# Chunk 2 turned by DMA, rest products in pairs, and the second residual made by ScalarE and GpSimd

## The reference

```python
xn = layernorm(x)
# branch 1, per sequence
w = exp(tanh(((xn @ W + b) @ xn.T) / (|s - t| + eps)));  w[s, s] = 0
attn = (w / (w.sum(-1) + eps)) @ xn
# branch 2, per token: two of eight experts, and a shared one
scores = sigmoid(xn @ gate_w.T);  sel = top_k(scores + expert_bias, 2)
h_e = relu((score_e * xn) @ w_up[e].T) ** 2          # hidden size 176, bf16
ffn = sum over sel of h_e @ w_down[e].T + relu(xn @ shared_up.T) ** 2 @ shared_down.T
out = x + attn + ffn
```

## Time and profile before

| | us |
|---|---|
| median of 3 runs | 116.38 (115.9 to 116.49) |
| profiled execution | 116.35 |
| its span, first to last instruction | 114.5 |
| TensorE busy | 108.1 |
| VectorE busy | 100.7 |
| ScalarE busy | 88.4 |
| GpSimd busy | 71.0 |

### The profile page before, as it was taken

The page is one execution under the profiler, slowest core; times in us unless marked ns, Lnnn a source line. Parts: engine busy times, 40 slices in busy tenths (PEclk is TensorE's granted clock), DMA queues, the critical chain, the costliest instruction groups (busy, mean ns, idle before and its releaser), DMA issues.

```text
span 114.5 us, 2792 instructions
## 1 busy us (share of the span) xinstructions
PE 108.1 (94%) x898; PEld 82.6 (72%) x898; DVE 100.7 (88%) x319; ACT 88.4 (77%) x136; POOL 71.0 (62%) x134
## 2 busy tenths in 40 slices
PE   3987999969999999999999999999999999999990
PEld 3955558757787695878588777869588767859790
DVE  6979989998798989999899989998999689989751
ACT  3454899986748996888788797879788887899550
POOL 6538953599939489677969498776967610516000
PEclk9999999999999999999999999999999999999999
DMA  3999306656772769999698939893988659887983
GB/s 108 311 258 300 115 0 121 130 109 124 139 137 51 185 119 190 169 217 120 113 213 191 143 75 208 168 217 58 173 174 217 126 105 127 174 198 132 109 234 95
DMA packets 52191, 17.62 MB, mean 154 GB/s; under 512 B 49233, under 2 KB 50129, under 8 KB 52177
## 3 DMA queue, kind: packets, MB, share of 16 engines
q1 hardware_dynamic: 51600, 16.49, 72.6%
q0 software_dynamic: 288, 0.72, 3.4%
q10 hardware_dynamic: 288, 0.23, 0.6%
HBM read 3.84 MB, written 2.10 MB: 52 GB/s over the span
## 4 chain that ended last, share of the span: by engine, by line
PE 87%; DMA 5%; ACT 2%; DVE 2%; issue 1%; POOL 1%; DVEq 0%; POOLq 0%
PE out_ps L1089 16%; PE h_ps L1040 13%; PE dots L996 11%; PE side L1017 10%; PE out_ps L1077 6%; DMA hiddenT<-hidden 5%; PE out_ps L1071 5%; PE small L981 5%; PE side L1030 4%; PE out_ps L1119 4%; PE small L952 4%; PE h_ps L1053 2%; ACT hidden L563 1%; PE small L933 1%; PE side L972 1%; PE small L961 1%
## 5 line engine op out<-in xcount | busy, mean ns | idle before, releaser
L754 DVE SCALAR_TENSOR_TENSOR gated<-h_ps,gates 128x1408 bf16<-128x1408 f32 x28 | 45.2, 1615 | 3.3 <-PE h_ps L1040 2.3
L563 ACT ACTIVATE hidden<-gated 128x1408 bf16<-128x1408 bf16 x29 | 39.7, 1378 | 3.0 <-DVE gated L754 2.9
L1089 PE MATMUL out_ps<-downT,hiddenT 128*128 128x128 bf16 x341 | 22.8, 219 | 0.9 <-DMA hiddenT<-hidden 0.9
L1089 PEld LDWEIGHTS out_ps<-downT,hiddenT 128*128 128x128 bf16 x341 | 20.8, 98 | 3.3 <-DMA hiddenT<-hidden 1.1
L1040 PE MATMUL h_ps<-upT,xnTb 128*128 128x512 bf16 (+1 forms) x84 | 21.3, 362 | 0.0
L1017 PEld LDWEIGHTS side<-xn,probs 128*128 128x128 f32 x120 | 15.1, 191 | 1.5 <-issue 0.5
L1017 PE MATMUL side<-xn,probs 128*128 128x129 f32 x120 | 16.1, 276 | 0.0
L996 PE MATMUL dots<-projT,xnT 128*128 128x256 f32 x60 | 15.4, 380 | 0.0
L996 PEld LDWEIGHTS dots<-projT,xnT 128*128 128x128 f32 x60 | 11.0, 190 | 4.4 <-issue 1.7
L1040 PEld LDWEIGHTS h_ps<-upT,xnTb 128*128 128x128 bf16 x84 | 7.1, 98 | 9.6 <-issue 3.2
L357 POOL TENSOR_SCALAR_AFFINE_SELECT probs<-probs 128x256 f32<-128x256 f32 x16 | 6.6, 411 | 10.9 <-ACT probs L512 10.8
(11 more groups left out here) (122 smaller groups left out, 184.3 us busy)
## 6 DMA issues: line engine op xcount, KB each, us to landing
x_sb<-in_x SPq DMA_DIRECT2D x7, 256.0 KB, 8.1
out_y<-final SPq DMA_DIRECT2D x7, 256.0 KB, 2.3
hiddenT<-hidden SPq DMA_TRANSPOSE x31, 3.6
upT<-in_up POOLq DMA_DIRECT2D x1, 352.0 KB, 6.9
downT<-in_down POOLq DMA_DIRECT2D x1, 352.0 KB, 7.9
late_sb<-in_late SPq DMA_DIRECT2D x1, 192.0 KB, 5.2
x_sb<-in_x SPq DMA_DIRECT2D x1, 128.0 KB, 2.4
x_sb<-in_x ACTq DMA_DIRECT2D x1, 128.0 KB, 2.6
```

The source lines that it names most:

```text
L563: a.activation(hidden[:, t, :], gated[:, t, :], ACT.Square).then_inc(squared, 1)
L754: v.scalar_tensor_tensor(out=gated[:, t, :].rearrange("p (e h) -> p e h", e=E), in0=h_ps[:, 0:NH].rearrange("p (e h) -> p e h", e=E), scal ...
L1089: last = t_.matmul(out_at(c, t), hiddenT[:, c % 2, t, j, :], downT[:, j, :], start=(t == 0 and j == 0 and c < LAST), stop=((t >= 2 or c == ...
```

## The change

Four parts.

1. Chunk 2 joins the chunks that are turned by DMA: `BY_DMA` becomes a list, `transpose_x(2)` and `take_xT(2)` go, `split(2)`, `turn_planes(2)` and `merge(2)` come.
2. In the first chunks `down_tile(0, 0)` and `(0, 1)` move down in TensorE's order, behind `up_tile(1, 0)` and behind `shared_down_rest(0)`.
3. The rest products of chunks 2 and 3, 4 and 5, 6 and 7 are run in pairs: those of the odd chunk one pass earlier, into the upper half of the output banks. The odd chunk's main product takes the place of its rest products and does the waiting for the finished chunk before.
4. For chunks 1 to 6 the second sequence's residual is made like chunk 0's: ScalarE scales (`scale_second`, behind `square(c, 1)`), GpSimd adds x (`add_second_x`, behind `make_gates`), and VectorE's `attend(c)` goes. `shared_main(c)` then waits for `second_scaled`. Chunk 7 keeps VectorE's way, and `attend(7, 1)` moves behind the last up product.

```diff
-        BY_DMA = 4
+        BY_DMA = (2, 4, 5, 6, 7)
...
+        def pair_second(c):
+            return c >= 3 and c % 2 == 1
+
+        def pair_first(c):
+            return pair_second(c + 1)
+
-        def out_bank(h):
-            return out_ps[:, h * CH:h * CH + 2 * P]
+        def out_bank(c, h):
+            at = h * CH + (2 * P if pair_second(c) else 0)
+            return out_ps[:, at:at + 2 * P]
...
 # SP
+            turn_planes(2)
             for k in range(1, NCH):
                 turn(k - 1, 0)
...
 # GpSimd
-            def add_second_x():
-                pool.wait_ge(second_scaled, 1)
-                g.tensor_tensor(resid[:, 0, 2:4, :], scaled[:, 1, :, :], x_sb[:, 0, 2:4, :], ALU.add
+            def add_second_x(c):
+                pool.wait_ge(second_scaled, c + 1)
+                wait(pool, final_ready, 2 * (c - 1))
+                g.tensor_tensor(resid[:, c % 2, 2:4, :], scaled_second[:, c % 2, :, :], x_sb[:, c, 2:4, :], ALU.add
                                 ).then_inc(second_resid, 1)
...
             normalize(2, 3, 4)
+            split(2)
             mask(0, 0)
             mask(0, 1)
             square_rest(0)
+            merge(2)
             square_shared(0)
...
             add_x(1)
+            add_second_x(1)
             square_shared(1)
...
                 if f < NCH:
                     make_gates(f)
+                if c < LAST:
+                    add_second_x(c)
                 square_shared(c)
                 if f < NCH:
                     mask(f, 0)
...
 # ScalarE
-                if c == 1:
-                    act.wait_ge(second_resid, 1)
                 wait(act, first_resid, c - 1)
...
-            def scale_second():
-                act.wait_ge(attn_step, 4)
+            def scale_second(c):
+                act.wait_ge(attn_step, 2 * (Q * c + 1) + 2)
+                wait(act, second_resid, c - 1)
                 for t in range(2):
-                    last = a.activation(scaled[:, 1, t, :], attend_bank(0, 1)[:, t * (D + 1):t * (D + 1) + D],
+                    last = a.activation(scaled_second[:, c % 2, t, :],
+                                        attend_bank(c, 1)[:, t * (D + 1):t * (D + 1) + D],
                                         ACT.Identity, scale=rownorm[:, 1, t:t + 1])
                 last.then_inc(second_scaled, 1)
...
-            take_xT(2)
             take_pair(1)
...
             square(1, 1)
+            scale_second(1)
             take_pair(2)
...
                 square(c, 0)
                 square(c, 1)
+                scale_second(c)
                 take_proj(f)
...
 # VectorE
             route_mark(2)
-            attend(1)
             finish(0, 0)
...
                 attend_norm(c, 1)
-                attend(c)
                 finish(o, 0)
...
 # TensorE
                 elif c > 0:
-                    pe.wait_ge(attn_taken, c)
+                    pe.wait_ge(second_scaled, c + 1)
                 t_.matmul(shared_bank(c), supT, xnT[:, c % 4, :], start=True, stop=True).then_inc(sup_made, 1)
...
                 else:
-                    pe.wait_ge(final_ready, 2 * c)
+                    pe.wait_ge(final_ready, 2 * (c - 1) if pair_second(c) else 2 * c)
...
             def shared_down_main(c):
                 pe.wait_ge(sup_squared, c + 1)
+                if pair_second(c):
+                    pe.wait_ge(final_ready, 2 * c)
...
             dots(1, 1)
-            transpose_x(2)
             up_tile(0, 3)
             attend(0, 1)
-            down_tile(0, 0)
             rest(2)
             up_tile(1, 0)
+            down_tile(0, 0)
             attend(1, 0)
+            shared_down_rest(0)
             down_tile(0, 1)
-            shared_down_rest(0)
             transpose_exp(2)
...
                 up_tile(c, 0)
                 attend(c, 0)
-                shared_down_rest(o)
+                if pair_second(o):
+                    shared_down_main(o)
+                else:
+                    shared_down_rest(o)
+                if pair_first(o):
+                    shared_down_rest(o + 1)
                 rest(f)
                 up_tile(c, 1)
-                shared_down_main(o)
+                if not pair_second(o):
+                    shared_down_main(o)
                 down_tile(o, 2)
...
             up_by_bank(1)
             shared_down_rest(o)
+            shared_down_rest(c)
             shared_down_main(o)
             up_by_bank(2)
-            attend(c, 1)
             down_tile(o, 2)
             down_tile(o, 3)
             up_by_bank(3)
-            shared_down_rest(c)
+            attend(c, 1)
             shared_down_main(c)
```

More of the change, by code:

```diff
@@ L233, in turn_planes @@
                 sp.wait_ge(planes_split, merges(c))
-                wait(sp, xT_merged, merges(c - 2))
+                wait(sp, xT_merged, merges(c) - 2)
                 sp.dma_start_transpose(
-                    planesT[:, c % 2, :, :].rearrange("p h (t n) -> p (h t) n", n=P),
-                    planes[:, c % 2, :, :, :].rearrange("p h t d -> p (h t d)")
-                ).then_inc(planes_turned[c % 2], 16)
+                    planesT[:, plane_slot(c), :, :].rearrange("p h (t n) -> p (h t) n", n=P),
+                    planes[:, plane_slot(c), :, :, :].rearrange("p h t d -> p (h t d)")
+                ).then_inc(planes_turned[plane_slot(c)], 16)
             def store_last(h):
@@ L330, in split @@
                 pool.wait_ge(xn_ready, xns(c, TILES - 1))
-                wait(pool, planes_turned[c % 2], planes_count(c) - 16)
-                g.tensor_copy(planes[:, c % 2, :, :, :],
+                wait(pool, planes_turned[plane_slot(c)], planes_count(c) - 16)
+                g.tensor_copy(planes[:, plane_slot(c), :, :, :],
                               xn[:, c, :, 0:D].bitcast(U16).rearrange("p t (d h) -> p h t d", h=2)
@@ L341, in merge @@
                 g.tensor_copy(xnT[:, c % 4, :].bitcast(U16).rearrange("p (n h) -> p h n", h=2),
-                              planesT[:, c % 2, :, :]).then_inc(xT_merged, 1)
+                              planesT[:, plane_slot(c), :, :]).then_inc(xT_merged, 1)
             def narrow(c):
-                if c < BY_DMA:
-                    pool.wait_ge(xT_taken, c + 1)
+                if c not in BY_DMA:
+                    pool.wait_ge(xT_taken, taken(c))
                 else:
@@ L410, in _ @@
             square_first_chunk_end()
-            add_second_x()
+            add_second_x(0)
             mask(1, 1)
@@ L460, in take_xT @@
             def take_xT(c):
[L461 removed]
+                act.wait_ge(xT_made, taken(c))
                 wait(act, sup_made, c - 3)
@@ L589, in _ @@
             square(0, 2)
-            scale_second()
+            scale_second(0)
             relu_rest(2)
@@ L945, in rest @@
                     pe.wait_ge(first_half_taken, 1)
-                if c >= BY_DMA:
+                if c == 2:
+                    pe.wait_ge(expT_taken, 2)
+                elif c in BY_DMA:
                     pe.wait_ge(proj_taken, c)
+                if c in BY_DMA:
                     pe.wait_ge(xT_merged, merges(c))
                 for h in range(2):
-                    if 0 < c < BY_DMA or c == 0 and h == 1:
-                        pe.wait_ge(xT_taken, c + 1)
+                    if c in (1, 3) or c == 0 and h == 1:
+                        pe.wait_ge(xT_taken, taken(c))
                     last = t_.matmul(small[64 * h:64 * h + 64, 0:S], restT, xnT[:, c % 4, h * S:(h + 1) * S],
@@ L1070, in shared_down_rest @@
                         rows = slice(64 * h, 64 * h + 64)
+                        own_bank = c == LAST and 2 * h + i == TILES - 1
+                        bank_first = h == 1 and i == 0 and not pair_second(c)
                         t_.matmul(out_at(c, 2 * h + i), rest_hidden[rows, c % 4, i * P:(i + 1) * P],
-                                  sdown_tail[rows, :], start=((i == 0 and (h == 1 or c == LAST)) or (c == LAST and h == 1)), stop=False, skip_group_check=True)
+                                  sdown_tail[rows, :], start=(own_bank or bank_first), stop=False,
+                                  skip_group_check=True)
             def shared_down_main(c):
                 pe.wait_ge(sup_squared, c + 1)
+                if pair_second(c):
+                    pe.wait_ge(final_ready, 2 * c)
                 for t in range(TILES):
@@ L1089, in down_tile @@
                     last = t_.matmul(out_at(c, t), hiddenT[:, c % 2, t, j, :], downT[:, j, :],
-                                     start=(t == 0 and j == 0 and c < LAST),
+                                     start=(t == 0 and j == 0 and not pair_second(c)),
                                      stop=((t >= 2 or c == LAST) and j == KT - 1), skip_group_check=True)
```

25 lines of the change are left out of this document (13 added, 12 removed).

## The result

The changed kernel took 119.07 us, the median of four runs (118.75 to 119.2), against 116.37 for the kernel before beside it (115.9 to 116.49): a ratio of 1.0279, 95% interval 1.0227 to 1.0332. (The quotient of the two medians is 1.023, at the lower end of that interval; why the two differ is not on record.) That is slower by 2.7 us, where the forecast said 3.4 and 119.7. The profiled execution took 118.75 with a span of 117.0, so in the traces 2.5 us of span are to be found.

The account below looks back on a forecast made before the run. TensorE was taken to bound the kernel, with mask and `side` nearly late. Terms -0.65 + 2.65 + 1.56 - 0.2 = +3.36 us on the 114.5 span, plus 1.85, gave 119.7 us, 2.9% slower; range 116.9 to 121.0.

Parts of the forecast that it names:

- both links: `attend(f, 0)` waiting for GpSimd's mask and `shared_main(c)` for ScalarE's second scaling; both bind, chance 0.60, 118.2 to 121.0 us.
- ramp up to `attend(2, 0)`: First chunks: transposes gone -0.44, wait before second down product gone -0.89, `rest(2)` later +0.3; sum -1.0 us.
- loss on ScalarE in pass k = 3, with its second scaling: `scale_second(1)` ahead in ScalarE's queue takes back 0.35 us of the ramp's gain; `shared_main` 0.04 later.
- mask link: GpSimd's addition behind the gates costs 0.69 against 0.16 slack before `attend(f, 0)`: 0.53 a pass, 2.65 us in five.
- two passes with both rest blocks: Passes o = 2, 4: `rest(f)` and `shared_main` 0.43 later, plus 0.04 for the second scaling; 0.94 us for two.
- two passes with none: Passes o = 3, 5: `rest(f)` 0.25 later, TensorE's saved 0.64 waited away at `shared_main`, plus 0.04; 0.58 us for two.
- last chunk: `attend(7, 1)` behind the last up product, rest products ahead; VectorE's third gate limits the gain: -0.2 us (0 to -0.46).
- Not all of it survives: Chunk 1: `scale_second(1)` makes ScalarE gain only 0.35 of the ramp's 1.0 us, so -0.65 at `dots(3, 0)`.
- TensorE's busy time: Sign to look for in the profile after: TensorE's busy time down by about 1.0 us.
- A: Rival: TensorE stays the bound and the added waits hide; -1.9 us, 114.5 us; chance 0.12.
- B: Rival: only one link binds; mask alone +0.85, 117.2 us, or ScalarE alone +0.7, 117.1 us; chance 0.18.
- C: Rival: turn of `square(c, 1)` or planes' merge slips too, 0.3 to 0.5 a pass and ramp's 1.3; 122 us; chance 0.10.

Follow-up runs that it names:

- the ramp alone: Kernel before with only chunk 2 turned by DMA and the down tiles moved; 115.65 us, ratio 0.9983, and in a second run 115.71 us, ratio 0.9985.
- the spare addition: Kernel before plus one unused GpSimd addition per pass: behind the gates 118.6 us, ratio 1.0212; ahead of them 116.29 us, ratio 1.0028.
- without the mask link: Changed kernel with `add_second_x(c)` moved ahead of `make_gates(f)` in GpSimd's order, nothing else; 117.1 us, ratio 1.0101.

## Why the prediction was right

The direction and both links were right, and the size nearly; the sum was too high by 0.9 us against the trace. Of that, 0.41 is the start of the program, which no term holds and which differs by as much between the two traces of the ramp alone (9.37 and 9.80). The rest is mainly the loss in pass k = 3 and the passes without a rest block, both priced too high, and a gain in the last chunk that did not come. Term by term, forecast and trace of after:

| term | forecast, us | trace, us |
| --- | --- | --- |
| ramp up to `attend(2, 0)` | -1.0 | -0.96 |
| loss on ScalarE in pass k = 3, with its second scaling | +0.39 | +0.08 |
| mask link, five passes | +2.65 | +2.6 |
| two passes with both rest blocks | +0.94 | +0.88 |
| two passes with none | +0.58 | +0.36 |
| last chunk | -0.2 | -0.04 |
| start of the program | 0 | -0.41 |

The fifth mask's last 0.1 falls behind `attend(7, 0)`, whose block takes 1.16; it is counted with the mask here.

**The mask: right.** Forecast 0.53 a pass. Between dots and attend the starts are 0.41 further apart, and 0.1 falls into the next stretch, 0.52 in all. The kernel before with the spare addition behind the gates pays as much, and with the addition ahead of them nothing. The forecast's sentence that GpSimd idles before the gates and not behind them was the whole of the matter. "Idle some 0.5 before every `attend(f, 0)`" is 0.24 on TensorE and 0.69 on its weight loads, and neither is the loss; the distance between starts shows it.

The Trainium skill's rule on two-input additions ("GPSIMD Engine Reference", section "Engine selection") holds here as far as it goes: 0.73 on GpSimd against 0.41 on VectorE, a factor of 1.8 where the rule says about 2. But the slower addition cost nothing in one place and 0.52 a pass in the other, and VectorE's freed time bought nothing: it was busy 2.7 us less and its gates waited 6.3 us for TensorE's up tiles, where they had waited 2.3.

**The pairs: right in sign and pattern, too high in the passes without a rest block (0.58 for 0.36).** The passes alternate 13.43 and 13.17 where 13.5 and 13.3 stood. The mechanism was half told. The forecast let all 0.64 of TensorE's saving arrive at `shared_main` and be waited away there, behind the second scaling. With the residual on VectorE, 0.40 of it is already gone on the way, at `attend(c, 1)` and `project(f)`; the second scaling takes the rest and some more: the pass goes from 12.22 with the residual on VectorE to 13.18, of which 0.52 is the mask and 0.44 the second scaling. In a pass with both blocks the second scaling adds nothing (12.98 + 0.52 against 13.43). So the idle time before `shared_main` was 0.62 on the weight loads, not 0.9, and 0.16 to 0.17 in the passes with both blocks. The 0.04 that the sum holds in every pass for the later weight load is in no trace: without the pairs the second scaling costs a pass nothing.

**"Not all of it survives": right on ScalarE's queue, wrong on the way to TensorE and on the size.** The forecast took 0.35 off the ramp's gain, since ScalarE would come later to `exp_logits(3)` by an estimated 0.65. ScalarE's `square(1, 2)`, behind the second scaling in the same queue, is later by that: the transpose of its tile is issued 25.69 after `dots(0, 0)` in after and 25.01 in the ramp alone. But `exp_logits(3)` itself starts only 0.09 later (29.06 and 28.97), and nothing is lost there. The loss is at `down_tile(1, 2)`, which needs that transpose: 0.08 in after, so that nearly all of the ramp's 0.96 stayed. In the other five kernels with a second scaling in chunk 1 the same place lost 0.06 to 0.07 twice, 0.24, 0.42 and 0.44. In all six the transpose took 4.7 to 5.0 from issue to landing, and 3.5 to 3.8 in the seven traces without that scaling, which lost nothing there. Issued at 34.79 in after and 3.8 long, it would have landed at 38.6, well ahead of `down_tile(1, 2)` at 39.5; so it takes the longer landing too, and why that is longer is open.

**The last chunk: failed in size.** The third gate did become what `up_by_bank(3)` waits for, as named. TensorE behind `attend(7, 0)`, in after:

```profile
108.95 0.55 PE L1072 MATMUL h_ps<-upT,xnTb 128*128 128x512 bf16 x2 [0.23 <-DVE gated L791]
```

That wait and the rest products in front of it left next to nothing of the -0.2: the stretch behind `attend(7, 0)` is 15.12 long, 0.1 of it the mask's, and 15.06 before.

**TensorE's busy time: failed as a sign to look for.** It was to fall by 1.0 and rose by 1.6, since a wait first takes up the overlap between rows and a block that waited is recorded longer: of the mask's 0.52 a pass only 0.25 shows as idle time.

**The ramp's gain: seen in each trace, not in the medians.** It is there in all nine traces with the new ramp against all four with the old, and yet in the two kernels that have it alone the time falls by 0.2%, each with no difference inside its interval. In their passes, 0.1 and 0.3 go again in the last one, in the second of them at a late transpose, as shown. Where the remainder goes is open: the start alone varies by 0.75 us over the traces here. Nor is it known that every execution of the kernel before waits the 0.89: its shortest execution had a span of 113.0, where the traced ones with its ramp have 114.2 or more.

**The rivals.** A (TensorE stays the bound) is excluded by the waits. B, one link only, is excluded by them too, and each link was taken away by itself: without the mask link 1.0% over the kernel before is left, some 1.2 us where the forecast had +0.7, and without the pairs 2.0%, some 2.3 us where it had +0.85, or 1.45 without the 0.6 that the pairs were to save. That 117.1 stands in the forecast and in the first of these medians is luck, as the kernel before was faster beside it. C, a third link, is there in a small size, at `attend(c, 1)` and `project(f)`, but it takes away a saving and adds no time.

## What to carry to other kernels

Before work is moved to an engine that has idle time, look where that idle time lies in the engine's own order: the same 0.7 us is free ahead of the wait that starts a chain and costs 0.5 a pass behind it. Time saved on a full engine counts only in the stretch where it is still what ends last; here, work that was shifted between alternate passes made one late and had the other wait, and without the pairs the kernel was faster. Price every link by the slack between the two rows that meet there, and judge by distances between starts, not by busy shares.

## What the runs showed of the hardware

A product block whose weight load was waited for is recorded from about the start of the load: eight products took 1.16 us where they take 1.05 to 1.06, and the load and the first product both start at 75.30. With the overlap of 0.17 between rows that follow without a wait, this is why the idle time in brackets (0.25) and the lost time (0.52) differ by a factor of two.

The DMA transposes of `hidden` take 3.6 to 3.7 us from issue to landing in the median, and single ones up to 5.3. At two places the long landing belongs to the kernel and not to the execution. The transpose that the second down product of chunk 0 needs took 5.2 in all four traces with the old ramp, with a wait of 0.89 or 0.90, and 3.6 to 3.9 in the changed kernel and the two traces of the ramp alone. The one that `down_tile(1, 2)` needs took 4.7 to 5.0 in all six kernels with a second scaling in chunk 1 and 3.5 to 3.8 in the other seven traces. What makes it long is not shown. Other waits come and go: the last pass of the ramp alone is 0.33 longer in one trace, with a recorded wait of 0.15 for a transpose, and 0.11 longer in the other, with none recorded.
